# Routed rows written back by index as they are finished, and read back plainly, in place of plain stores and indexed gathers

## The reference

```
x1 = layernorm(x + attention(x))             # 16 heads of 8 dims, rope, causal
shared = (silu(x1 @ sw1) * (x1 @ sw3)) @ sw2 # every token, hidden width 256
logits = x1 @ router_w.T + experts_bias      # 8 experts
rw, sel = top_k(logits, 2); rw = softmax(rw)
routed = sum over the 2 chosen experts e of rw_e * ((silu(x1 @ w1[e]) * (x1 @ w3[e])) @ w2[e])
out = layernorm(x1 + routed + shared)
```

## Time and profile before

| what | value |
|---|---|
| median of 3 runs | 616.53 us |
| the profiled execution, its own time | 615.48 us |
| its span, first to last instruction | 613.5 us |
| mean granted TensorE clock | 0.917 |
| busy: PE / DVE / ACT / POOL | 82% / 76% / 51% / 53% of the span |
| indirect DMAs on GpSimd | 64 scatters, 64 gathers |
| plain stores of routed tiles | 69 on SyncE's queue, 23 on ScalarE's |

### The profile page before, as it was taken

How to read it: one execution, slowest core, us unless ns; L and a number is a source line. 1 busy time by engine, 2 the same in 40 slices (tenths; PEclk the granted TensorE clock), 3 DMA queues, 4 the chain that set the end, 5 groups by cost and what they waited for, 6 DMA issues and landing times.

```text
span 613.5 us, 14589 instructions
## 1 busy us (share of the span) xinstructions
PE 500.8 (82%) x4278; PEld 335.3 (55%) x4278; DVE 467.0 (76%) x1938; ACT 313.0 (51%) x752; POOL 323.5 (53%) x533
## 2 busy tenths in 40 slices
PE   6568889899879789999999989999899985497300
PEld 3212344456544249856675666767568984497200
DVE  3498999999978886998898999999826872165334
ACT  3106766766646645566666746575774432153100
POOL 5405634834668730268646765366865456405254
PEclk9786999999979789999999999999999998699755
DMA  5863322042526147744756483572456575697111
GB/s 167 230 199 113 115 80 80 3 130 80 165 72 191 57 127 210 247 144 140 230 166 188 128 238 104 139 212 90 127 149 183 159 215 142 183 306 244 39 52 51
DMA packets 77390, 90.40 MB, mean 147 GB/s; under 512 B 10241, under 2 KB 59393, under 8 KB 77313
## 3 DMA queue, kind: packets, MB, share of 16 engines
q1 hardware_dynamic: 69616, 78.79, 43.0%
q0 software_dynamic: 4096, 8.40, 4.6%
q10 hardware_dynamic: 3600, 2.30, 1.4%
HBM read 67.16 MB, written 21.89 MB: 145 GB/s over the span
## 4 chain that ended last, share of the span: by engine, by line
PE 55%; DVE 17%; issue 10%; POOL 4%; ACT 4%; DMA 4%; SPq 3%; another core or an unknown queue 2%; ACTq 0%; POOLq 0%; DVEq 0%
PE ps L1229 16%; PE ps L1135 10%; PE ps L1241 9%; PE ps L1091 8%; DVE sums L1311 6%; POOL yg L904 3%; PE ps L1077 2%; DVE acc L1459 2%; ACT probs L948 2%; PE ps L1146 2%; PE ps L1213 2%; DVE negmax L1311 1%; SPq L801 1%; PE ps L1084 1%
## 5 line engine op out<-in xcount | busy, mean ns | idle before, releaser
L1311 DVE CUSTOM_DVE_ANT_0 sums<-ps,mask_sb 128x384 bf16<-128x384 f32 (+3 forms) x512 | 218.0, 483 | 28.3 <-PE ps L1091 27.6
L948 ACT ACTIVATE probs<-ps 128x512 f32<-128x512 f32 x320 | 171.4, 610 | 54.5 <-PE ps L1091 44.9
L882 POOL TENSOR_SCALAR_AFFINE_SELECT probs<-probs 128x256 f32<-128x256 f32 (+1 forms) x320 | 113.0, 365 | 115.8 <-ACT probs L948 108.1
L1091 PE MATMUL ps<-stack 64*128 64x512 bf16 (+3 forms) x1024 | 120.2, 314 | 25.5 <-DMA stack<-parts_scratch 7.5
L1229 PE MATMUL ps<-xgT,w_tile 128*128 128x128 f32 x736 | 99.7, 284 | 0.8 <-ACT ot L984 0.6
L1436 DVE SCALAR_TENSOR_TENSOR gate<-th,ps 128x256 f32<-128x256 f32 x124 | 51.5, 416 | 63.3 <-ACT th L1012 55.8
L1229 PEld LDWEIGHTS ps<-xgT,w_tile 128*128 128x128 f32 x736 | 90.4, 196 | 9.1 <-issue 6.8
L904 POOL DMA_INDIRECT yg<-rows_out,slot x64 | 61.5, 961 | 60.2 <-DVE acc L1459 25.0
L1091 PEld LDWEIGHTS ps<-stack 64*128 64x128 bf16 x1024 | 42.7, 96 | 83.9 <-issue 21.2
L1135 PE MATMUL ps<-probs,va 128*32 128x512 f32 (+3 forms) x1024 | 84.0, 473 | 5.0 <-POOL probs L882 3.4
L894 POOL DMA_INDIRECT rows_in<-x,slot x64 | 63.0, 984 | 35.1 <-DVE slot L1428 23.9
(11 more groups left out here) (108 smaller groups left out, 582.6 us busy)
## 6 DMA issues: line engine op xcount, KB each, us to landing
w_tile<-in_experts SPq DMA_DIRECT2D x92, 384.0 KB
stack<-parts_scratch SPq DMA_DIRECT2D x106, 128.0 KB
parts_scratch<-parts SPq DMA_DIRECT2D x16, 384.0 KB
xg<-rows_in SPq DMA_DIRECT2D x20, 256.0 KB
rows_out<-y_routed SPq DMA_DIRECT2D x69, 64.0 KB
rows_in<-zeros SPq DMA_DIRECT2D x14, 192.0 KB, 3.8
x_t<-in_x SPq DMA_DIRECT2D x8, 256.0 KB, 3.0
x_r<-in_x SPq DMA_DIRECT2D x8, 256.0 KB
```

What stands on the lines that cost most here:

```text
L882: pool.affine_select(out=area, in_=area, compare_op=ALU.is_ge, fill=0.0, base=0, pattern=pattern, channel_multiplier=-1).then_inc(masked, 1)
L948: act.activation(probs[:, (s * NB + v) % PRING, :], bank("scores", s, v), ACT.Exp, scale=SCALE)\
L1091: return pe.matmul(into[:, at:at + width], here[:, stationary, at_s:at_s + P], here[:, moving, at_m:at_m + width], start=True, stop=True)
L1311: ins = dve.tensor_tensor_reduce(sums[:, use % 2, at:at + w], bank("max", s, u)[:, at:at + w], mask_sb[:, S - w:S], -1.0, 3.0e38, ALU.add, ...
```

## The change

`rows_out` is now in the order of the tokens, with the two choices of a token in neighbouring rows. Each finished tile is written there by one indirect DMA (`put_rows`, GpSimd), rows of padding being dropped by the bounds check; a sequence's results come back with one plain 256 KB load (`load_y`, SyncE). The destination of a row is worked out from two numbers that travel with the row: `x1`, `rows_in` and `xg` have 130 columns in place of 128, the column `D` a mark of the token's place and `D + 1` the first expert. `store_rows`, its ScalarE form `store_last`, and `gather` are gone. The weight ring `WRING` is 7 in place of 8. The planner's distances are `GAPS` of 1300 and 1000 ns (scatter; other groups and last) and 1000 and 1000 ns (put), against 2600 ns before for both kinds, 1300 for the last group's scatters and 0 for the last gathers; `HOLD` is 500 in place of 1000. All numbers in `AT` and `LATER` are others, so the order of every engine's line may differ. The diff, cut to its core:

```diff
-    scatter=22.57, routed_last=16.6, routed_last_but_one=-1.09, apart_last=1.11, stored=8.33, ... (AT)
+    scatter=15.21, routed_last=11.47, routed_last_but_one=-0.73, apart_last=0.07, stored=1.98,
+    load_y=9.47, load_y_last=47.34, dest=-17.73, combine_last=13.47, ... (AT; LATER likewise)
-GAP, GAP_LAST, GAP_END = 2600, 1300, 0
-HOLD = 1000
+GAPS = dict(scatter=(1300, 1000), put=(1000, 1000))
+HOLD = 500
-    XRING, WRING, YRING, HRING, TRING = 3, 8, 4, 3, 3
+    XRING, WRING, YRING, HRING, TRING = 3, 7, 4, 3, 3
...
-        x1 = sb("x1", [P, X1RING, T, D]); x1T = sb("x1T", [P, 2, S])
+        x1 = sb("x1", [P, X1RING, T, D + 2]); x1T = sb("x1T", [P, 2, S])
-        rows_in = [nc.dram_tensor(f"rows_in{n}", [NT * P, D], F32).ap() for n in range(2)]
-        rows_out = [nc.dram_tensor(f"rows_out{n}", [NT * P, D], F32).ap() for n in range(2)]
+        rows_in = [nc.dram_tensor(f"rows_in{n}", [NT * P, D + 2], F32).ap() for n in range(2)]
+        rows_out = [nc.dram_tensor(f"rows_out{n}", [2 * MOST * P, D], F32).ap() for n in range(2)]
...
-        def store_rows(eng, i):
-            ...
-            eng.dma_start(rows_out[g % 2][k * P:(k + 1) * P, :], y_routed[:, use % YRING, :])\
-              .then_inc(rows_stored[use % YRING], 16)
...
             def load_rows(g, q):
...
+                    sp.wait_ge(dest_done, dest_use[(gone, qone)] + 1)
...
+            def load_y(s):
+                g = group_of[s]
+                for n in range(YRING):
+                    sp.wait_ge(rows_stored[n], 16 * stores_of(n, g))
+                if s > 0:
+                    sp.wait_ge(combined, s)
+                r0 = 2 * S * SORTED[g].index(s)
+                sp.dma_start(yg[:, :, :, :].rearrange("p t r d -> p t (r d)"),
+                             rows_out[g % 2][r0:r0 + 2 * S, :].rearrange("(t p r) d -> p t (r d)", p=P, r=2))\
+                  .then_inc(gathered[s % 2], 16)
...
-            def gather(g, s, t, r):
-                ...
+            def put_rows(i):
+                _, g, k = STEP[i]
+                use = routed_use[(g, k)]
+                count = 2 * S * len(SORTED[g])
+                pool.wait_ge(*drained("down", i))
+                pool.wait_ge(dest_done, dest_use[(g, k // XQ)] + 1)
+                if i == first_put[g] and g >= 2:
+                    for s in SORTED[g - 2]:
+                        pool.wait_ge(gathered[s % 2], 16 * (s // 2 + 1))
                 pool.indirect_dma_start(
-                    ...
+                    out=rows_out[g % 2][0:count, :], out_offset=bass.IndirectOffsetOnAxis(ap=dest[:, g % 2, k:k + 1], axis=0),
+                    in_=y_routed[:, use % YRING, :], in_offset=None, bounds_check=count - 1, oob_is_err=False)\
+                    .then_inc(rows_stored[use % YRING], 16)
...
+                dve.tensor_copy(x1[:, s % X1RING, :, D], column["mark"][:, s * T:s * T + T])
+                dve.tensor_copy(x1[:, s % X1RING, :, D + 1], topf[:, :, 0])
...
+            def destinations(g, q):
+                use, n = rows_use[(g, q)], min(XQ, TILES[g] - XQ * q)
+                ...
+                link(dve.tensor_tensor(same[:, 0:n], xg[:, use % XRING, 0:n, D + 1], expert_f[:, g % 2, XQ * q:XQ * q + n],
+                                       ALU.is_equal), dest_chain, 2 * done + 1)
+                link(dve.scalar_tensor_tensor(out=dest_f[:, 0:n], in0=same[:, 0:n], scalar=-1.0, in1=xg[:, use % XRING, 0:n, D],
+                                              op0=ALU.mult, op1=ALU.add), dest_chain, 2 * done + 2)
+                dve.tensor_scalar(dest[:, g % 2, XQ * q:XQ * q + n], dest_f[:, 0:n], float(past + 1), None, ALU.add)\
+                   .then_inc(dest_done, 1)
...
             def combine(s, c):
                 rows = tiles_at(c)
-                if s < B - 1:
-                    dve.wait_ge(gathered[s % 2], 16 * 2 * T * (s // 2 + 1))
-                else:
-                    for t in range(rows.start, rows.stop):
-                        dve.wait_ge(gathered_last[t], 32)
+                dve.wait_ge(gathered[s % 2], 16 * (s // 2 + 1))
```

More of the change, by code:

```diff
@@ L28 @@
 SORTED = [[0, 1], [2, 3], [4, 5], [6, 7]]
[L32 to L40, removed]
@@ L43 @@
[L43 to L49, removed]
[4 rows of a table removed]
[L54 to L59, removed]
@@ new lines @@
+AT = dict(load_y=9.47, load_y_last=47.34, dest=-17.73, weight_ahead=-0.3, tables=-6.94, fill=24.41, fill_step=-38.24,
+          routed0=-1.26, routed1=-4.22, routed2=-23.18, stay=0.1, values=2.11, v=8.26, rows1=-5.73, maxima1=-7.27,
+          heads_T0=-11.52, heads_T1=4.15, out_T=-35.57, out=-44.23, ln1_stats=-5.89, ln1=8.38, x1_T=-44.62,
+          router=0.2, weights=10.81, load_residual=-6.81, load_x=-61.59, x_T=-57.69, project0=-50.7, project1=-54.29,
+          rope=-69.33, rest=-56.07, low=7.81, store_parts=-24.41, stack0=-52.02, stack1=-14.54, rows0=-11.33,
+          maxima0=-10.09, count=-25.04, rank=-7.32, scatter=15.21, scatter_step=0.23, shared=23.03, shared_step=2.75,
+          routed=36.92, margin=1.19, apart=0.15, T=-5.93, tanh=6.08, glu=4.54, down=3.61, stored=1.98,
+          weight_late=32.31, combine=-8.39, lull_from=-29.99, lull_to=35.02, lull=1.61, routed_last_but_one=-0.73,
+          routed_last=11.47, apart_last=0.07, combine_last=13.47)
@@ L412, in needs @@
                 return found + [("sp", "load_rows", s - 2, q) for q in range(loads_in.get(s - 2, 0))]
-            if kind == "gather":
-                found = [(*stored_by(s), step_of[("routed", s, k)]) for k in range(TILES[s])]
-                return found + [("dve", "combine", key[1] - 1, T)]
+            if kind == "put":
+                _, g, k = STEP[s]
+                found = [("act", "down", s), ("dve", "dest", g, k // XQ)]
+                return found + [("sp", "load_y", n) for n in (SORTED[g - 2] if g >= 2 else ())]
             if kind == "shared_rows":
@@ L442, in needs @@
             return [("sp", "stack", 0, 1, len(SLOTS) - 1)]
-        if kind == "store_rows":
-            _, g, k = STEP[s]
-            found = [("act", "down", s)]
-            return found + [("pool", "gather", g - 2, *tile) for tile in tiles_in.get(g - 2, ())] if k == 0 else found
+        if kind == "load_y":
+            g = group_of[s]
+            found = [("pool", "put", step_of[("routed", g, k)]) for k in range(TILES[g])]
+            return found + [("dve", "combine", s - 1, T)]
         return [("dve", "ln2", *key)]
@@ L574, in build_block @@
             max_use[key] = len(max_use)
+        if kind == "dest":
+            dest_use[key] = len(dest_use)
+    for kind, key in line("pool"):
+        if kind == "put":
+            first_put.setdefault(STEP[key[0]][1], key[0])
     for i, key in enumerate(STEP):
@@ L640, in build_block @@
         column = {}
-        for name, wide in (("earlier", P), ("ones", P), ("iota", E), ("thr", MOST), ("below", E), ("upto", E), ("tile", NT * E)):
+        for name, wide in (("earlier", P), ("ones", P), ("iota", E), ("thr", MOST), ("below", E), ("upto", E), ("tile", NT * E), ("mark", B * T)):
             column[name] = consts_sb[:, at:at + wide]
```

131 lines of the change are left out of this document (70 added, 61 removed), and 8 rows, old and new, of the table LATER.

## The result

The changed kernel takes 647.35 us (median of 4 runs, 646.49 to 649.32), the kernel before 617.01 beside it (615.56 to 618.25): ratio 1.0497 [1.0463, 1.0532], 30 us slower. 604 was forecast. The profiled execution took 646.96 us with a span of 645.2, against 615.48 and 613.5.

A forecast was written before the change was run, and what follows sets the result against it. TensorE was taken as the bound from 250 to 495 us, with three open places after. Span: 613.5 - 15.5 - 3 + 0 + 6 = 601.0, with execution and median offsets 604 us; own range 598 to 611, 8 in 10 593 to 618.

The forecast's parts named there:

- Part 1: From the last copy to the span's end: 39.5 us shrinks to 23.9, a saving taken as 15.5.
- Part 4: The body, to 495 us: added VectorE and GpSimd work and indirect DMAs cost +6 us, bounds 0 and +17.
- the term of the indirect DMAs: In the body: each added indirect DMA costs TensorE 0.14 us, 4.2 us for 30.
- Rival 1: From 495 to 574 us: puts run into one another and the last scatters in bursts, 627 us; chance 0.13.
- part 3: Wait for the last group's sorted rows: earlier load against puts among the scatters, 0 in sum, bounds -4 and +10 us.
- part 2: The last group's 23 tiles: 1.70 us a tile, 42 us in all, saving 3; bounds saving 9, loss 11.
- a burst starves of puts: Argument against bursts from 495 to 574 us: a put needs a TensorE completion itself, so a burst ends; no size.
- leave gaps on their own: Last group's tiles: puts come one per tile and wait for its copy, supporting 1.70 us a tile.
- Case 4: At the end: the last put lands later than a gather's 2.5 us, 2 us more, 606 us; chance 0.10.
- Used up: Body and last scatters: added GpSimd and VectorE work costs +12 in place of +6, puts +5, 615 us; chance 0.13.
- B: Theory of the experiments: the loss comes from work added to GpSimd and VectorE and puts' waits in GpSimd's line.
- The wider rows: Transfers of rows: 1.6% more bytes, 0 by themselves; a skill rule would make part 3's load some 1 us longer.

The follow-up runs named there:

- 9: Changed kernel without indirect DMAs (plain stores, unsorted plain copies), GpSimd keeping the waits that stand before puts: 598.79 us, ratio 0.9710 to the kernel before.
- 10: As 9, with three small memsets, some 1.1 us, on GpSimd in place of each of the 156 indirect DMAs: 603.44 us, ratio 0.9759.
- 8: As 2, with VectorE's 24 `destinations` left out too: 594.07 us, ratio 0.9622 to the kernel before.
- 2: Changed kernel in its order without any indirect DMA: plain stores by ScalarE for puts, plain unsorted copies by SyncE for scatters: 597.71 us, ratio 0.9703.
- 1: Changed kernel with puts replaced by plain stores from ScalarE, order unchanged, scatters kept: 620.70 us, ratio 1.0057 to the kernel before.
- 5: Kernel before with the change (put, destinations, load_y) in the last group alone, groups 0 to 2 stored and gathered as before: 615.05 us, ratio 0.9969.
- 13: Changed kernel, each of the 156 indirect DMAs replaced in place by a plain DMA from GpSimd, rows unsorted, on another chip: 590.48 us, ratio 0.9815.
- 14: Kernel before in its order without indirect DMAs, rows copied unsorted by SyncE, no results fetched, on the chip of 13: 589.94 us, ratio 0.9823.
- 11: Kernel before with distances of 1300 ns (1000 for the last group's scatters), its own `HOLD` of 1000 kept: 646.69 us, ratio 1.0488.
- 17: Kernel before with 3200 ns planned between indirect DMAs in place of 2600, nothing else changed: 628.99 us, ratio 1.0213.
- 15: As 5, but with the change in groups 2 and 3, group 2's puts planned 2600 ns apart, on the chip of 13: 626.45 us, ratio 1.0416.
- 3: Changed kernel with distances of 2600 ns (1300 in the last group) for scatters and puts, and `HOLD` of 1000: 648.23 us, ratio 1.0533.
- 16: Changed kernel with scatters planned 2600 ns apart (1300 in the last group), puts and `HOLD` as changed: 643.84 us, ratio 1.0448.
- 4: Kernel before with distances of 1300 ns (1000 for the last scatters) and `HOLD` of 500, stores and gathers kept: 637.36 us, ratio 1.0362.
- 7: The order of 3 (its distances and `HOLD`) with no indirect DMA, replaced as in 2: 617.41 us, ratio 0.9983 to the kernel before.
- 6: Changed kernel, order unchanged, with three small GpSimd memsets behind each of the 48 scatters of groups 0 to 2: 677.20 us, ratio 1.0973.
- 12: Kernel before with `HOLD` of 500 in place of 1000, its own distances kept: 623.34 us, ratio 1.0101.

## Why the prediction was wrong

**Part 1, the end, held**: 13.8 saved of 15.5, 25.7 us for 23.9. The last put starts 1.67 us after the copy for 0.1, lands 0.4 sooner than taken, and the first load takes 0.4 more; small gaps make the rest.

**Part 4, the body, is the step that failed**: +35.6 for +6, bounds 0 to +17. Its small terms stand: GpSimd's time 3 us (9 and 10), `destinations` 5 us where 3 were let through (8), the puts' waits 1 or nothing (9). What was mis-sized is the term of the indirect DMAs, 4.2 us. It took 0.14 us from two rates of the last group's tiles (16.5 us for 10.2 tiles is 1.62, not 1.60, so 0.16 and 4.9 us; nothing hangs on it) and multiplied it by the 30 DMAs that are added. So the 48 scatters of groups 0 to 2, which stand in both kernels, cost nothing in it, though the diff halves their planned distance and the trace after shows 26.0 us for 56.9. The runs give 45 us for all 156 indirect DMAs (10 to after); with GpSimd's time in it, 23 by the scatters (2 to 1) and 27 by the puts (1 to after). The mechanism was seen, at 563.12, and its price per DMA was read where they cost little to TensorE's rate, not as a held completion. That the whole of it goes through held completions is not shown (see what stays open). In the body one held completion can stop TensorE, ScalarE and VectorE together, for 3.9 us at 170.88 and for 5.7 before 451.16.

**Rival 1 named the mechanism and lost by place and price.** It had bursts from 495 to 574 us only, "the body its 6 as before". There the loss was +4.7 and +5.2, less than its 9 (part 3) and 11 (part 2). The argument that a burst starves of puts was wrong twice: the scatters need no TensorE completion, and puts of tiles already done are queued (5).

**Part 2**: 50.0 us for 42. By the working's own form, less 2.7 for the first tile's way, that is 2.06 us a tile, not 1.70, and inside its bound of 2.32; the kernel before has 1.83 by the same form. The claim that puts "leave gaps on their own" fell. **Part 3**: +4.7, inside its bounds of -4 and +10. Its sentence that 1000 for 1300 ns gives nothing was about the last group only; the 2600 of the others is in no term of the sum.

**Case 4** did not come: the put landed in 2.08 us. **Used up** (B) is worth 0.005 by experiment 10, 0.008 by 8. **The wider rows**: no run isolates them. In experiments 13 and 14, on one chip, the load of sorted rows lands in 3.9 us (rows of 520 bytes) and in 3.3 us (512 bytes) in the median, beside other traffic.

The Trainium skill (DMA: Bandwidth & Descriptors, Issuing engines are not separate DMA queues) says that issuing on another engine saves only the sequencer's time, the DMAs running on the same 16 engines. By that rule experiment 2 should give back about what experiments 9 and 10 add, 3 us. It gives back 49 us (1.0497 to 0.9703), so for indirect DMAs the runs decide against it. For plain DMAs issued by GpSimd no run tells, since experiment 13 stands on the chip on which indirect ones held nothing either.

**What stays open.** How much of the 30 us between the kernels is the scatters' distance and how much the puts' being there: 11 reaches all of it without a put, but 17 warns that a changed distance disturbs the plan by 0.02. From what distance on a completion is no longer held: every run that changed it changed the order or the masks' time as well. What in the chip holds it is not in the trace, nor why nothing is held in experiment 15; plain DMAs from GpSimd on one of the other chips were not tried. How much of the 45 us passes through held completions is open too: unexplained waits fall to 25 us in 3 and 22 in 16, and the time stays within 0.005. No version tried that computes everything gains over 0.5%; experiment 5, 0.9969, is the best.

## What to carry to other kernels

Before adding indirect DMAs, or letting them follow each other more closely, count the distances between their starts in every stage, not only where they are exposed, and look for waits without a releaser on ScalarE and VectorE that follow a finished matmul. Price such a burst by what one held completion stops, not by a rate per DMA, and measure on more than one chip: here one of them showed no held completion. Look also at which engine's copies wait for the indirect DMAs' landing (experiment 15). A planner's distance is no free knob either: with its other numbers fitted to 2600 ns, both 1300 and 3200 lost.

## What the runs showed of the hardware

- While indirect DMAs of GpSimd start some 1.3 to 1.6 us apart, completions of TensorE can reach ScalarE and VectorE several us late: 4.0 us at 174.12, and 6.8 at 450.51 in the longest wait of the changed kernel (8.5 us, its matmuls end at 443.74). TensorE's next matmul then waits for the bank.
- Unexplained waits were 84 us in the changed kernel with 83 close distances, 58 with 85 (11) and 88 (4), 12 with 43 (before), and 0 without indirect DMAs (2, 7, 8, 9, 10, 14). With nearly equal counts of 51 to 53 they were 18 to 32 (3, 6, 12, 17), and 0 on the chip of experiment 15.
- 156 plain DMAs on the same queue, 90 of them under 1.7 us apart, held nothing (13), on the chip on which the indirect ones held nothing (15). Form and issuing engine are not told apart.
- A plain DMA occupies GpSimd 0.55 us, an indirect one 0.97 to 0.99. GpSimd's time itself was cheap: 156 times 1.1 us of memsets cost 0.5% (10).
- A 512 KB load landed in 3.39 us at the quiet end, beside 3.0 for the 256 KB of the earlier trace rows; the eight such loads of experiment 10 took 3.4 to 6.6, 4.4 in the median.
